# First cross attention of a fused decoder: four heads to a step, and products that nobody reads

## What is computed

```python
def _L0_xattn_ref(x, cond, wq, bq, wkv, bkv, wp, bp):
    q = _qdq(x) @ _qdq(wq).T + bq
    kv = cond @ wkv.T + bkv
    k, v = jnp.split(kv, 2, axis=-1)
    q = q.reshape(B, N, H, Dh)      # H = 16, Dh = 32
    k = k.reshape(B, M, H, Dh)
    v = v.reshape(B, M, H, Dh)
    scale = 1.0 / np.sqrt(Dh)
    attn = jax.nn.softmax(jnp.einsum('bnhd,bmhd->bhnm', q, k) * scale, axis=-1)
    o = jnp.einsum('bhnm,bmhd->bnhd', attn, v).reshape(B, N, C)
    out = _qdq(o) @ _qdq(wp).T + bp
    return out
...
x = x + _L0_attn_ref(...)
x = x + _L0_xattn_ref(_layernorm(x, axis=-1), ctx_2048, ...)
x = x + _L0_ffn_ref(x, ...)
```

## Time and profile before

| | us |
|---|---|
| median of 3 runs | 2844.05 |
| lowest and highest | 2843.87, 2846.97 |
| the profiled execution | 2845.22 |
| its span, first to last instruction | 2843.4 |
| first scores of `cross1` to its last group of scores | 256.5 |
| from there to the end of the segment | 29.3 |

### The profile page before, as it was taken

How to read it: one execution, slowest core, us unless ns; L and a number is a source line. 1 busy time by engine, 2 the same in 40 slices (tenths; PEclk the granted TensorE clock), 3 DMA queues, 4 the chain that set the end, 5 groups by cost and what they waited for, 6 DMA issues and landing times. The chain is left out here.

```text
span 2843.4 us, 49717 instructions
## 1 busy us (share of the span) xinstructions
PE 2622.6 (92%) x15595; PEld 2128.3 (75%) x15596; DVE 1698.7 (60%) x3165; ACT 1130.6 (40%) x2442; POOL 770.5 (27%) x790
## 2 busy tenths in 40 slices
PE   8999799979899989889998898998999999899998
PEld 7888666548778877768876687776777788788887
DVE  4537745558877656566665567774444436566664
ACT  2113255532243323455544133665544422344443
POOL 3213100004333324423333200650000003245555
PEclk9999855569989989989999798999999989999999
DMA  5453121104542135477775431444122031566664
GB/s 189 153 145 97 38 78 58 58 4 154 171 126 62 34 129 163 121 206 226 195 219 120 115 80 44 148 137 150 55 79 63 31 117 46 163 159 160 163 149 80
DMA packets 289282, 332.97 MB, mean 117 GB/s; under 512 B 147445, under 2 KB 202693, under 8 KB 287312
## 3 DMA queue, kind: packets, MB, share of 16 engines
q1 hardware_dynamic: 217904, 252.57, 28.7%
q0 software_dynamic: 20640, 51.74, 9.5%
q10 hardware_dynamic: 50560, 26.34, 3.2%
HBM read 233.86 MB, written 96.72 MB: 116 GB/s over the span
## 5 line engine op out<-in xcount | busy, mean ns | idle before, releaser
L898 PE MATMUL e_psum<-e_up_hi,hT_hi 128*128 x672 | 245.7, 366 | 22.4 <-DVE hT_lo L867 15.3
L900 PE MATMUL e_psum<-e_up_hi,hT_lo 128*128 x672 | 237.4, 353 | 0.0
L899 PE MATMUL e_psum<-e_up_lo,hT_hi 128*128 x672 | 237.0, 353 | 0.0
L898 PEld LDWEIGHTS e_psum<-e_up_hi,hT_hi 128*128 128x128 f32 x672 | 127.8, 190 | 45.4 <-issue 34.6
L1565 POOL TENSOR_TENSOR self_a_p<-self_a_p,self_a_mx 112x448 f32<-112x448 f32 x96 | 96.0, 1000 | 206.3 <-DVE self_a_mx L1622 206.3
L794 ACT ACTIVATE e_gate<-e_psum 128x352 f32<-128x352 f32 (+1 forms) x86 | 44.4, 516 | 259.6 <-PE e_psum L900 259.2
L873 DVE TENSOR_TENSOR hT_lo<-e_psum,hT_hi 128x256 fp32r<-128x256 f32 (+2 forms) x138 | 55.7, 435 | 142.3 <-ACT hT_hi L812 138.9
L1656 ACT ACTIVATE self_a_p<-self_a_p 112x448 f32<-112x448 f32 x128 | 71.6, 575 | 167.2 <-POOL self_a_p L1565 114.4
L1947 PEld LDWEIGHTS joint_psum<-x_v,joint_a_pt 125*112 125x112 f32 (+1 forms) x1024 | 121.2, 180 | 21.8 <-issue 14.0
L900 PEld LDWEIGHTS e_psum<-e_up_hi,hT_lo 128*128 128x128 f32 x672 | 127.8, 190 | 11.9
L899 PEld LDWEIGHTS e_psum<-e_up_lo,hT_hi 128*128 128x128 f32 x672 | 127.8, 190 | 10.1
(11 more groups left out here) (565 smaller groups left out, 7441.8 us busy)
## 6 DMA issues: line engine op xcount, KB each, us to landing
e_up_raw<-in_L_ffn_w SPq DMA_DIRECT2D x64, 512.0 KB, 8.3
e_up_raw<-in_L_ffn_w SPq DMA_DIRECT2D x64, 352.0 KB, 4.0
e_dn_raw<-in_L_ffn_w SPq DMA_DIRECT2D x16, 1024.0 KB, 15.7
q_all<-p_p_t_stage ACTq DMA_DIRECT2D x56, 256.0 KB
e_dn_raw<-in_L_ffn_w SPq DMA_DIRECT2D x16, 512.0 KB, 5.9
x_q<-q_all SPq DMA_DIRECT2D x8, 896.0 KB
v_ctx<-front_c_v_stage SPq DMA_DIRECT2D x24, 250.0 KB
x_others<-k_ctx SPq DMA_DIRECT2D x8, 750.0 KB
```

The source lines that it names most:

```text
L898: pe.matmul(out, lhs[0], rhs[0], start=k == 0, stop=False)
L899: pe.matmul(out, lhs[0], rhs[1], start=False, stop=False)
L900: return pe.matmul(out, lhs[1], rhs[0], start=False, stop=k == n_k - 1)
```

## The change

A step has four heads instead of two (W = 4), and the ring of exponentials holds two steps. TensorE's scores come first in a step, the four heads one after the other on four row groups and in four banks. They wait until all exponentials of the step before are done: each bank serves one step at a time. The transposes that follow are those of the step before (LT = 1), and ahead of those of three heads of four stands a product of the identity with the identity, 128 columns, into the unused end of the same bank; nobody reads it. Maxima and biases stay in pairs, two of them a step. ScalarE copies the first two turned heads ahead of the exponentials and the other two behind them. The order gets an `o` for every `a`, and places 90 and 130 to 137 now lie later in a shorter list.

```diff
-        dh, n_items, W, group = 32, 16, 2, 4
+        dh, n_items, W, group = 32, 16, 4, 4
...
-        RING, LT, LP = 3 * W, 2, 2
+        RING, LT, LP = 2 * W, 1, 2
...
+        PAD = 384
...
+                for i in items(step):
+                    b, h = i // n_items, i % n_items
+                    if h == 0:
+                        reuse(pe, qk_in[b % 2], (b + 1) // 2 * 16 * (1 + n_k))
+                    reuse(pe, exp_done, W * step)
+                    pe.matmul(ps[0:T, s_banks[i % N_S], 0:S], q[rows_of(h), b % 2, h // group, :],
+                              k[rows_of(h), b % 2, h // group, :], start=True, stop=True).then_inc(s_done, 1)
                 for t in items(step, LT):
                     pe.wait_ge(exp_done, t + 1)
                     reuse(pe, pt_ready, t - N_T + 1)
+                    if t % W < 3:
+                        pe.matmul(ps[:, t_banks[t % N_T], PAD:512], core.ident[:, :], core.ident[:, 0:512 - PAD], start=True, stop=True)
...
-                for i in items(step):
-                    b, h = i // n_items, i % n_items
-                    if h == 0:
-                        reuse(pe, qk_in[b % 2], (b + 1) // 2 * 16 * (1 + n_k))
-                    reuse(pe, exp_done, i - N_S + 1)
...
-                    dve.wait_ge(s_done, i + W)
                     reuse(dve, exp_done, i - RING + W)
...
+                    for u in range(0, W, 2):
+                        dve.wait_ge(s_done, i + W)
+                        dve.tensor_reduce(mx[:, r + u:r + u + 2], ps[0:T, bank + u:bank + u + 2, 0:S], AX.X, ALU.max).then_inc(mx_ready, 1)
...
-                for t in items(step, LT):
-                    act.wait_ge(t_done, t + 1)
...
+                for t in items(step, LT)[0:2]:
+                    copy_turned(act, t)
...
+                for t in items(step, LT)[2:]:
+                    copy_turned(act, t)
...
-                    order = attention_order(a, o, 16, 16, gap=1.9)
+                    order = attention_order(a, o, 8, 8, gap=0.95)
```

More of the change, by code:

```diff
@@ L1741, in tensor @@
                     last.then_inc(t_done, 1)
-                for i in items(step):
-                    b, h = i // n_items, i % n_items
-                    if h == 0:
-                        reuse(pe, qk_in[b % 2], (b + 1) // 2 * 16 * (1 + n_k))
-                    reuse(pe, exp_done, i - N_S + 1)
-                    pe.matmul(ps[0:T, s_banks[i % N_S], 0:S], q[rows_of(h), b % 2, h // group, :],
-                              k[rows_of(h), b % 2, h // group, :], start=True, stop=True).then_inc(s_done, 1)
                 yield
@@ L1778, in vector @@
                     i, r, bank = both[0], both[0] % RING, s_banks[both[0] % N_S]
-                    dve.wait_ge(s_done, i + W)
                     reuse(dve, exp_done, i - RING + W)
-                    dve.tensor_reduce(mx[:, r:r + W], ps[0:T, bank:bank + W, 0:S], AX.X, ALU.max).then_inc(mx_ready, 1)
-                    dve.wait_ge(mx_ready, step + 1)
-                    dve.tensor_scalar(neg[:, r:r + W], mx[:, r:r + W], -scale, None, ALU.mult).then_inc(neg_ready, 1)
+                    for u in range(0, W, 2):
+                        dve.wait_ge(s_done, i + W)
+                        dve.tensor_reduce(mx[:, r + u:r + u + 2], ps[0:T, bank + u:bank + u + 2, 0:S], AX.X, ALU.max).then_inc(mx_ready, 1)
+                        dve.wait_ge(mx_ready, (i + u) // 2 + 1)
+                        dve.tensor_scalar(neg[:, r + u:r + u + 2], mx[:, r + u:r + u + 2], -scale, None, ALU.mult).then_inc(neg_ready, 1)
                 yield
@@ L1794, in vector, with copy_turned @@
                 yield
+        def copy_turned(act, t):
+            act.wait_ge(t_done, t + 1)
+            reuse(act, pv_done, (t - PT) // group + 1)
+            src = ps[0:key_chunks[0], t_banks[t % N_T], 0:nch * T].rearrange("p (i t) -> p i t", i=nch)
+            act.copy(pt[0:key_chunks[0], t % PT, :, :], src).then_inc(pt_ready, 1)
         def scalar(act):
@@ L1799, in scalar @@
             for step in range(n_all + LE):
-                for t in items(step, LT):
-                    act.wait_ge(t_done, t + 1)
-                    reuse(act, pv_done, (t - PT) // group + 1)
-                    src = ps[0:key_chunks[0], t_banks[t % N_T], 0:nch * T].rearrange("p (i t) -> p i t", i=nch)
-                    act.copy(pt[0:key_chunks[0], t % PT, :, :], src).then_inc(pt_ready, 1)
+                for t in items(step, LT)[0:2]:
+                    copy_turned(act, t)
                 b = closed(step, LP + 1, n_steps)
@@ L1811, in scalar @@
                     b, h, r = i // n_items, i % n_items, i % RING
-                    act.wait_ge(neg_ready, step + 1)
+                    act.wait_ge(neg_ready, i // 2 + 1)
                     reuse(act, t_done, i - RING + 1)
```

## The result

The changed kernel takes 2798.63 us (median of 4 runs, 2798.36 to 2802.27) against 2844.18 of the kernel before: ratio 0.9841, 95% interval 0.9824 to 0.9858. That is 45.5 us less; the forecast was 38 less. Its profiled execution has a span of 2800.2 us, 43.2 under the 2843.4 of the earlier trace rows.

What follows compares the result with a forecast made beforehand. TensorE, mostly at 1.2 GHz, bounds the first cross attention. At a 0.7 share of 2.4 GHz a batch takes 27.9 us; 209 plus 38.7 for the end makes 248 instead of 285.8, so 2806 us, range 2772 to 2850.

Steps and rivals of the forecast that it cites:

- plain step at 2.4 GHz: First cross attention, four heads without output-part extras: a chain of scores, copies and exponentials, 5.5 us a step.
- more for `oT_hi`: Once a batch, this copy of turned oq stands ahead of ScalarE's exponentials, which start at 5.0 us: +1.9 us.
- more for `by_value`: Once a batch, this 0.53 us copy stands ahead of the exponentials: +0.5 us.
- more for late maxima: VectorE's chain from addition to norm takes 5.3 us against a gap of 2.9, delaying the next maxima: about +0.75 us.
- share of time at 2.4 GHz: Share of the cross attention with the clock up, taken between 0.18 as before and the self attention's 1.00: 0.7.
- from there to the end: Last scores to the last subtraction: 38.7 us instead of 29.3, as the last output part starts later; 9.4 us lost.
- Without the clock the change loses: If the cross attention stays at 1.2 GHz, TensorE remains the bound and a batch takes 37.2 us, against 33.1 before.
- rival 2: Clock stays as it is, at 2.4 GHz for 0.18 of the time: 10 us slower, 2854 us; chance 0.11 with anything less.
- part `f`: Weight part whose last four steps stand among the last output steps; VectorE's addition waits behind its third load: about 2 us.
- sum of 37.2 us: TensorE's batch at 1.2 GHz in the changed kernel: scores, transposes, unread products, values and 6 us of output part.
- rival 3: Four row groups run two and two, not at once: 32 us more at the share 0.7, 2838 us; chance 0.06.
- rival 1: The clock holds at 2.4 GHz throughout the cross attention: 58 us less, 2786 us; chance 0.22.

Runs made afterwards that it cites:

- wait filled: Changed kernel, with TensorE filling the wait of a new batch's values for VectorE with twelve more unread products: 2787.37 us, ratio 0.9805.
- early norm: Changed kernel, with the output part's addition and norm moved one half-step earlier by the order alone: 2776.19 us, ratio 0.9759.
- early norm without unread products: Changed kernel with addition and norm a half-step earlier and the unread products taken out: 2785.67 us, ratio 0.9800.
- turn and products early too: Changed kernel with addition and norm, and also the turn of quantised rows and the products, a half-step earlier: 2777.97 us, ratio 0.9773.

## Why the prediction was right, step by step

| | forecast | measured |
|---|---|---|
| scores of four heads at 2.4 GHz, us | as two, 0.89 | 0.90 |
| an unread product at 2.4 GHz, us | 0.4 | 0.22 to 0.24 |
| an unread product at 1.2 GHz, us | 0.65 | 0.3 |
| plain step at 2.4 GHz, us | 5.5 | 4.94 |
| plain step at 1.2 GHz, us | 7.8 | 6.8 |
| more for `oT_hi`, us | 1.9 | 1.65 |
| more for `by_value`, us | 0.5 | 0.44 |
| more for late maxima, us | 0.75 | 3.9 |
| batch at 2.4 GHz, us | 25.2 | 25.15 (wait filled) |
| share of time at 2.4 GHz | 0.7 | 0.78 |
| batch as it runs, us | 27.9 | 26.7 to 27.6 |
| to the first scores of the last step, us | 209 | 200.3 |
| from there to the end, us | 38.7 | 38.3 |

**The clock counts: shown.** Work added to the old kernel's bound engine made that kernel 30 us faster, with the clock at 0.89 instead of 0.59. The forecast share was an estimate between two far ends; 0.78 is (0.89 - 0.5) / 0.5. That it came out so near is in part luck: the clock was low for the first 17 us of the segment and behind the six long waits, which the forecast did not see, and with these waits gone the clock of the early norm is 0.95.

**"Without the clock the change loses": not borne out.** It rests on 0.65 us for an unread product at 1.2 GHz. Measured are 0.3, as a plain step there takes 6.76 us and without its three products 5.91. The forecast's terms make that step 7.8 us, and its sign of steps above 8 us at the low clock did not show. The kernel before took 7.59 us for the same four heads. So the price of rival 2, 10 us slower at the old clock, was too high too; no run held the changed kernel at that clock.

**The price of the product: too high.** The nearest row, 0.24 us, was right: twelve in a row took 2.84 us, and between transposes it is 0.22. The allowance for changing between transposes and products, which doubled it, has nothing to stand on. It is most of the 0.5 us by which the plain step was forecast too long, since the second head's copy ends at 2.66 us instead of 3.1, and the exponentials then take the 2.3 that were forecast.

**The late maxima: mis-sized.** In the step in which `by_value` comes but no norm yet, the second batch's, the step is 5.38 us, 0.44 over 4.94. With the norm it is 9.26: another 3.9. The forecast had the delay of the maxima right (5.3 us against a gap of 2.9, so 2.4 late, and 2.4 by the timeline) but priced it at 0.75. The exponentials start 4.65 us after the scores instead of 2.56, which is 1.6 more beside the 0.44 of `by_value`; part of this is that the plain step's exponentials start sooner than forecast, so that less of the delay is hidden. It had also left out the other half, 2.3 us from the last exponential (469.2) to the next scores (471.48): the evacuation is queued behind maxima and scaling on VectorE, the next batch's values wait for its bank, and the next scores stand behind these values. Third, the wait drops the clock. The run with the early norm shows the first two gone, that with the filled wait the third.

**Two errors cancel.** Four plain steps of 0.5 us too much and a long step of 3 too little (2.4 with the wait filled) make a batch of 25.2 that is right for wrong reasons. Most of the 9 us by which the forecast of the stretch was too long lie in its first ten steps: they took 55 us, where 27.9 us a batch less 6.5 gives 63. No norm stands in them, so they have the short steps and not yet the long one.

**The end: right in its sum.** 9.0 us were lost, 9.4 forecast, but by two errors that cancel. Quantising begins 20.9 us after the last scores (19.6 forecast), and the 2 us for part `f` did not come: from quantising to the end it takes 0.3 us more than before.

**Slips in the working, none of which moves the forecast.** From the first to the last pair of scores of the kernel before are 63 pairs, 7.875 batches and not 7.75, so a batch took 32.6 us and not 33.1. The sum of 37.2 us is 37.3. The 24 instructions of the values have 112 columns, so one after another they would need 2.5 us and not 2.9.

**Loads: right.** The table of waits names no load among what the scores waited for.

**The rivals.** Four row groups run at once, so rival 3 is out. The clock stayed neither up (rival 1) nor down (rival 2). The changed kernel's falls stand at waits of 3.6 us, and filling these removes the falls. The Trainium skill (TensorE: Matmul & The Clock Gate, "Why this matters for your kernels") warns of idle gaps between bursts of matmuls, and these two traces agree with it. As a rule by itself it is not enough here: the early norm without unread products waits 1.8 us at most from its third batch on and its clock is still 0.78, and the kernel before stayed at 0.50 for 27.3 us with TensorE busy all that time. I had put the waits of about 1 us against the rule and found nothing to fear; the 3.6 us one was there to be seen, had the queue behind the norm been followed to the evacuation.

## What to carry to other kernels

When the clock of TensorE is low in a stretch where it is busy, full-array products that nobody reads can be worth more than they cost: here 96 of them won 30 us in the old order, and their price is that of the nearest product in the trace. Price them at both levels of the clock before saying that a change loses without it. When an engine that was the bound becomes one that waits, follow the queue of the engine it waits for as far as the first thing that frees a bank, because a wait can cost twice: here 3.6 us of it in each of six batches cost as much again in the clock at and after it. Moving two phases in the order was then worth half as much as the whole change.

## What the hardware showed

TensorE at 94% busy ran at 0.59 of its clock, and at 79 to 85% busy at 0.89; in these runs the busy share of the engine does not tell the level. Waits of 1.7 to 1.8 us were followed by a fall six times out of six in the early norm without unread products, and once out of six in the kernel with them and with turn and products early too, where the waits stand in another step. Eight score products on four row groups take 0.90 us from the first start to the last end, four on two row groups 0.89. The same unread products that won 30 us in one order of work changed nothing measurable in another, in which a wait pulls the clock down, and won 9 in a third, in which it does not.
